# The last layer's loop: gathered rows turned ahead of made sender rows on TensorE, node weights centred in the loop's fourth step

## What is computed

```python
h = relu(layernorm(x))                                    # [3125, 64]
e = concatenate([h[src], h[dst], edge_attr], axis=-1)     # [53125, 192]
hidden   = relu(e @ msg_W1 + msg_b1)                      # [53125, 128]
messages = relu(hidden @ msg_W2 + msg_b2)                 # [53125, 64]
agg = segment_sum(messages, dst)                          # [3125, 64]
y = relu(concatenate([h, agg], -1) @ node_W1 + node_b1) @ node_W2 + node_b2
y = (y - mean(y)) * rsqrt(var(y) + 1e-5) * ln_scale + ln_offset
out = x + h + y
```

## Time and profile before

| | us |
|---|---|
| median of 3 runs (lowest, highest) | 1332.59 (1330.99, 1334.54) |
| the profiled execution, its own time | 1327.6 |
| its span, first to last instruction | 1325.8 |
| busy: TensorE matmuls | 1006.6 |
| busy: VectorE | 830.9 |
| busy: GpSimd | 592.2 |
| busy: ScalarE | 452.6 |
| mean granted TensorE clock (1 is 2.4 GHz) | 0.862 |

### The profile page before, as it was taken

How to read it: one execution, slowest core, us unless ns; L and a number is a source line. 1 busy time by engine, 2 the same in 40 slices (tenths; PEclk the granted TensorE clock), 3 DMA queues, 4 the chain that set the end, 5 groups by cost and what they waited for, 6 DMA issues and landing times.

```text
span 1325.8 us, 24512 instructions
## 1 busy us (share of the span) xinstructions
PE 1006.6 (76%) x6145; PEld 618.1 (47%) x6145; DVE 830.9 (63%) x2605; ACT 452.6 (34%) x1035; POOL 592.2 (45%) x763
## 2 busy tenths in 40 slices
PE   3788887996667767667696787777787878777685
PEld 2566553553444545445355444434444534444443
DVE  8988877357645556757657554565555555555556
ACT  3677771011434333334013232232232323222232
POOL 6533330000665666654003656555555555555550
PEclk9677778998887788877797899999888998999997
DMA  2000006001111111100523533333333333333331
GB/s 54 2 0 0 0 0 243 1 1 22 24 23 19 20 21 22 21 19 17 168 63 75 138 81 79 76 76 76 77 73 77 75 71 77 75 73 78 72 75 34
DMA packets 145110, 72.80 MB, mean 55 GB/s; under 512 B 111917, under 2 KB 136698, under 8 KB 144922
## 3 DMA queue, kind: packets, MB, share of 16 engines
q1 hardware_dynamic: 127224, 54.98, 16.0%
q0 software_dynamic: 16448, 16.88, 6.9%
q10 hardware_dynamic: 1378, 0.22, 0.1%
HBM read 59.66 MB, written 12.35 MB: 54 GB/s over the span
## 4 chain that ended last, share of the span: by engine, by line
PE 41%; another core or an unknown queue 20%; issue 16%; DVE 12%; ACT 6%; DVEq 2%; POOL 1%; ACTq 1%; DMA 1%; SPq 1%; POOLq 0%
PE seg L1628 10%; PE big L1658 5%; PE big L1552 4%; PE seg L1683 4%; PE seg L1755 3%; PE big L1791 3%; PE seg L1802 2%; ACT A L1345 2%; PE seg L1566 2%; PE big L1781 1%; ACT A L1466 1%; PE seg L1696 1%; ACT A L1472 1%; PE seg L1823 1%
## 5 line engine op out<-in xcount | busy, mean ns | idle before, releaser
L1221 POOL DMA_INDIRECT A<-table,idx x338 | 327.3, 968 | 260.6 <-ACT idx L1317 154.2
L1221 POOL DMA_INDIRECT pair<-table,idx x176 | 176.2, 1001 | 126.8 <-ACT idx L1317 65.0
L1755 PE MATMUL seg<-A 128*128 128x384 f16 (+1 forms) x624 | 137.6, 370 | 44.5 <-issue 19.1
L1466 ACT COPY A<-big 128x512 f32<-128x512 f32 x104 | 61.1, 587 | 249.7 <-remote 156.7
L1345 ACT CAST A<-big 128x500 f32 x208 | 125.4, 603 | 48.0 <-PE big L1557 25.9
L1791 PE MATMUL big<-A 128*128 128x512 f32 x208 | 114.1, 631 | 33.6 <-ACT A L1466 28.3
L2033 DVE COPY A<-seg 128x512 f32<-128x512 f32 x52 | 36.0, 691 | 162.3 <-remote 150.6
L1683 PE MATMUL seg<-A,cur 128*64 128x160 f32 x750 | 94.8, 353 | 46.0 <-issue 45.9
L1397 ACT COPY A<-big 128x500 f32<-128x500 f32 x120 | 66.5, 576 | 181.4 <-remote 113.8
L1755 PEld LDWEIGHTS seg<-A 128*128 128x128 f16 x624 | 60.3, 106 | 140.5 <-issue 91.0
L1658 PE MATMUL big<-A 128*128 128x300 bf16 x480 | 106.1, 367 | 18.8 <-issue 10.4
(11 more groups left out here) (307 smaller groups left out, 1809.6 us busy)
## 6 DMA issues: line engine op xcount, KB each, us to landing
A<-in_edge_attr_dram SPq DMA_DIRECT2D x103, 128.0 KB
A<-drel_flat SPq DMA_DIRECT2D x104, 126.0 KB
spilled_adjacency<-A SPq DMA_DIRECT2D x1, 7074.0 KB, 21.8
A<-spilled_adjacency SPq DMA_DIRECT2D x6, 1152.0 KB, 11.8
A<-table,idx POOLq DMA_INDIRECT x338
A<-pr_table SPq DMA_DIRECT2D x104, 31.5 KB
pair<-table,idx POOLq DMA_INDIRECT x176
A<-low_flat SPq DMA_DIRECT2D x78, 32.0 KB
```

The source lines that it names most:

```text
L1221: pool.indirect_dma_start(out=row(q, j), out_offset=None, in_=table, in_offset=bass.IndirectOffsetOnAxis(ap=idx[:, q, j:j + 1], axis=0)).t ...
L1466: nc.scalar.copy(x_t[:, r, :], big[:, r, :]).then_inc(x_t_ready[r], 1)
L1755: op = nc.tensor.matmul(made[:, 0:held.shape[2] * D], hot_low[:, u, m, :], held[:, k, :, :], start=(m == 0 and k == 0), stop=(m == 3 and k ...
```

## The change

TensorE's list of stages has `turn_rows` (group `s-1`) ahead of `make_rows` (group `s`); the other five stages keep their places. The six VectorE instructions that centre the node weights, and the raising of `node_weights_ready` behind them, move from ahead of the steps into a function that `steps` calls ahead of step 4 (`s == Q`, the first step of the second iteration). `steps` gets a parameter for it, which the other engines leave empty. No instruction is added, removed or changed in shape, and no wait is added or dropped.

```diff
-        def steps(eng, stages, between=lambda s: None):
+        def steps(eng, stages, between=lambda s: None, ahead=lambda s: None):
...
             for s in range(peeled * Q):
+                ahead(s)
                 one_step(0, s, 0, GROUPS)
...
-            steps(pe, [(0, make_rows), (1, turn_rows), (0, node_hidden), (6, window_sums), (2, hidden_sums), (4, turn_messages), (3, message_sums)])
+            steps(pe, [(1, turn_rows), (0, make_rows), (0, node_hidden), (6, window_sums), (2, hidden_sums), (4, turn_messages), (3, message_sums)])
...
-            for weights, many in ((nw2_sb, HID), (nb2_bc, P)):
-                link(dve.tensor_reduce(st_a[0:many, 0:1], weights, AX.X, ALU.add))
-                link(dve.tensor_scalar(st_c[0:many, 0:1], st_a[0:many, 0:1], 1.0 / D, None, ALU.mult))
-                link(dve.tensor_scalar(weights, weights, st_c[0:many, 0:1], None, ALU.subtract))
-            dve.sem_inc(ev("node_weights_ready"), 1)
+            def centre_weights(s):
+                if s != Q:
+                    return
+                for weights, many in ((nw2_sb, HID), (nb2_bc, P)):
+                    link(dve.tensor_reduce(st_a[0:many, 0:1], weights, AX.X, ALU.add))
+                    link(dve.tensor_scalar(st_c[0:many, 0:1], st_a[0:many, 0:1], 1.0 / D, None, ALU.mult))
+                    link(dve.tensor_scalar(weights, weights, st_c[0:many, 0:1], None, ALU.subtract))
+                dve.sem_inc(ev("node_weights_ready"), 1)
+
             steps(dve, [(1, receivers), (5, message), (0, senders), (4, plain_hots), (0, node_norm),
                         (7, add_windows),
                         (0, choose_rows)],
-                  between)
+                  between, centre_weights)
```

## The result

| | before | after |
|---|---|---|
| median (lowest to highest), us | 1331.79 (1329.96 to 1334.54) | 1343.56 (1343.09 to 1349.79) |
| profiled execution, its span | 1327.6, 1325.8 | 1343.6, 1341.8 |

The change makes the kernel slower: the ratio is 1.0097, with a 95% interval of 1.0063 to 1.0132. So the sign rests on the first chip and on the partial runs e1, e3 and e5; whether the size differs by the chip, or the four runs of each kernel on the first chip are too few to say, is not shown. The profiled execution before lies 4 us under its median and the one after at its median, so the 16.0 us between the two traces are more than the 11.8 between the medians.

The account below looks back on a forecast made before the run. GpSimd was taken as the bound: 260 gathers with spacing, 319 us, plus waits for `idx`. Shorter waits before seven gathers gave -8 us, the moved centring 0: 1332.6 - 8 = 1324.6, forecast 1325, range 1312 to 1352.

Parts of the forecast that it names:

- What holds the announcements: Last layer's loop: TensorE's semaphores are held while GpSimd issues gathers; some pass early, the rest a good microsecond after the run.
- The rule of the Trainium skill: A matmul's profiled end is an estimate, its semaphore pushed at PSUM's acknowledgement; lateness would be TensorE's own, sum zero.
- first in line at 0.8 us: Run of six gathers: group 0's turn ends 0.8 us after the first gather starts, today 2.3, and passes before the third.
- the wait is of the short kind: GpSimd's wait for row numbers before the seven gathers becomes about 2.75 us, as in five of 20 iterations today.
- the long kind: GpSimd's wait before the seven gathers in 14 of 20 iterations, priced at 3.54 us; shortening it was to save 0.77 each.
- the 11 us: Upper gain in the loop from shorter waits before the seven gathers: 0.77 us in 14 iterations, 0.4 in one; 8 taken.
- The second rival: Slower: group 1's made rows are held until the wait after the six gathers; 18 us lost, 1351 us, chance 0.20.
- sign of waits above 4 us ahead of the six: If group 1's made rows are held, GpSimd's waits before the six gathers, today some 3.2 us, grow above 4.
- In the six-gather round TensorE goes idle after that anyhow, so 0.45 us are covered: Made rows announced 0.45 us later in the run of six cost nothing, as the wait covers the delay.
- The rival's price: 5.25 us behind the wait less 3.84 slack, less 0.77 won: +0.6 per iteration; 0.9 taken, 18 us in 20, 1351.
- The centring: Six VectorE instructions, 1.65 us, moved from before the steps: 0 to -1.65 there, 0 to +1.65 in the new place; taken as 0.
- The startup up to 740 us should be the same within 1.7: Kernel's start, ahead of the loop: a check that it stays unchanged within 1.7 us.

Follow-up runs that it names:

- e1: Only TensorE's new order, turning ahead of making, with the centring left in its old place, against the kernel before: 1341.89 us, ratio 1.0052.
- e3: Turning first only in the step of group 1, where group 0 is turned, centring as before, against the kernel before: 1347.01 us, ratio 1.0086.
- e5: Turning first only from the sixth iteration on (loop and emptying), centring as before, against the kernel before: 1340.00 us, ratio 1.0042.
- e11: Kernel before plus 24 small GpSimd memsets behind the gathers of groups 0 and 2, against the kernel before: 1292.07 us, ratio 0.9808.
- e2: Only the centring moved, making still ahead of turning, against the kernel before: 1334.65 us, ratio 1.0008.
- e4: Turning first only in the steps of groups 2 and 3, centring as before, against the kernel before: 1340.92 us, ratio 1.0074.
- e18: Kernel before without group 1's making, pick, reduction and node matmul, or the waits for them, against the kernel before: 1334.06 us, ratio 1.0104.
- e15: Kernel before, unchanged, profiled a second time in one execution on another chip: 20 iterations take 442.4 us.

## Why the prediction was wrong

**The bound was right.** GpSimd's row adds up to the loop in both kernels, and the loop's loss is in the waits for `idx` (16.6 us, against 14.0 in all).

**What holds the announcements was read rightly.** Beside runs of gathers TensorE's announcements are held, and those that don't pass early come through 1.4 to 1.6 us after the last gather; e11 shows the same time with GpSimd at other work for part of it. The rule of the Trainium skill that the prediction set against it (Perfetto Trace Analysis, Tensor Engine Instruction) explains none of that: with no gathers due, as in the earlier trace rows, the lateness is gone.

**The step that failed** is the one with the turn "first in line at 0.8 us" and "the wait is of the short kind". The sum took the runs as given: it moved one announcement within today's run of six and left the run where it was, and 17 of 20 iterations have no such run any more. The three that are left show that the price was wrong too. The turn does pass there, ending 2.1 us after the run's start, but the waits behind are 3.24 to 3.35 us, 0.2 to 0.3 under the long kind and not 0.77. In the short round of before, the hidden sums were seen 1.2 us after the last gather; in the run shown above it is 1.6, and the relu and the row numbers stand behind that, whether the turn is copied or not. (The means give 3.54 - 2.75 = 0.79, which moves the 11 us by 0.3.) Counted against ScalarE's copies, group 0's turn is still over 1 us late in 15 of 20 iterations, where it was in 20 of 20. The prediction had named a different rhythm as what would make it wrong, but gave it no chance and no price.

**The second rival came nearest, at a chance of 0.20:** right in the sign and in the held rows. Its sign of waits above 4 us ahead of the six did not show. Made rows of group 1 were over 1 us late in none of 20 iterations before and in 15 after, up to 7.6 us. I set against it that rows ending 1.8 us into the run pass within 1.1 today. That took the passing for a matter of time in the run; it was a matter of what stands ahead in the line too, and the rival itself had said so. "In the six-gather round TensorE goes idle after that anyhow, so 0.45 us are covered" fell with it.

**The rival's price** was near, by the wrong place. It took the slack of the hidden sums at the end of the run of seven (3.84 us) and came to 0.6 to 0.9 us an iteration and 1351. Measured: 0.70 on the first chip and 1343.6 (the start is in it), 0.29 on the second. What is late first is group 1's row numbers, in the middle of that run, behind turn, making, hidden sums and two relus.

**The centring** was taken at 0, and e2's ratio of 1.0008 bears that out within 0.4%. "The startup up to 740 us should be the same within 1.7" was wrong: the first run grew to 17 gathers and the start by 6.1 us in one trace and 4.0 in the other. I looked only at who waits for the weights, not at which gathers an earlier turn may let on.

**The range** held the time by luck, by the rival's share of it; the sign did not. **Open:** whether the held rows alone make the new rhythm, why the loss was so unequal on two chips, by which path gathers hold announcements, and where e4's loss lies.

## What to carry to other kernels

Where a queue runs in bursts and its pauses are the bound, an edit can change the bursts themselves: follow the moved announcement and the one that it displaced through every consumer, up to the burst's next need, before pricing either. Where announcements came late beside another engine's gathers, the gain here lay in taking consumers out of their way (row numbers copied before the relus, 2.0%) or in giving them a gap (1.9%), not in their order. A rhythm is tested by switching the edit on in the loop alone and in the start alone.

## What the hardware showed beside that

Work added to the limiting engine made the kernel faster (e11). Work left out made it slower: e18 lacks the making, picking and reducing of one group in four and is 1.0% slower than before on the same chip. The granted clock went with it: 0.81 to 0.82 over the whole of e18's runs, 0.84 to 0.86 over those of before on that chip. The same view as above, first of e15 (before, unchanged, on another chip), then of e18:

```profile
828.10:1270.45 442.35, 344.47 (x1764) 196.30 (x1764) 255.26 (x783) 133.96 (x302) 252.33 (x260) 0.94 0.35 77
```

```profile
830.05:1287.50 457.45, 330.10 (x1559) 191.32 (x1556) 214.69 (x710) 132.09 (x300) 252.06 (x260) 0.82 0.32 74
```

TensorE has some 200 instructions less in the same 20 iterations, and its granted clock is 0.82 on average against 0.94: more of the stretch at the level of 1.2 GHz (0.50), less at 2.4 GHz. By an estimate from these means it is 36% of the stretch against 12%, as (1 - 0.82) / 0.5 and (1 - 0.94) / 0.5. Its busy time fell by 14 us only, and the waits for `idx` rose from 117.1 to 135.7. Whether the clock or the other runs of gathers (10 and 3 among them) made the loss, no run separates. e18's expectation, 0 to 25 us less than before, failed.
